# One reduction for the row maxima of both halves, on the ring of bank pairs: a four-layer decoder on one core

## What is computed

```
x = _layernorm(x + stage(x, ctx))
```

```
att = jnp.einsum('bhtd,bhsd->bhts', q, k) / math.sqrt(DH)
w = jax.nn.softmax(att, axis=-1)
```

## Time and profile before

| | |
|---|---|
| median of 3 runs | 1834.8 us (1828.02 to 1838.67) |
| the profiled execution | 1828.59 us, its span 1826.9 us |
| busy PE / DVE / ACT / POOL | 1387.8 / 1102.6 / 704.8 / 365.9 us |
| mean granted TensorE clock | 0.854 |
| DVE reductions of the row maxima (L1355) | 704 instructions, 411.7 us busy |
| exponentials of the pairs (L1766) | 352 instructions, 312.0 us busy |

### The profile page before, as it was taken

One profiled execution on the slowest core, in us unless ns is written; L12 is line 12 of the kernel. 1 busy time (PEld: TensorE's weight loads), 2 busy tenths in 40 slices (PEclk: granted clock), 3 DMA queues, 4 the chain that ended last, 5 costly groups with the idle time before them and its releaser, 6 DMA issues. The chain is left out here.

```text
span 1826.9 us, 25724 instructions
## 1 busy us (share of the span) xinstructions
PE 1387.8 (76%) x9530; PEld 662.0 (36%) x9530; DVE 1102.6 (60%) x2350; ACT 704.8 (39%) x988; POOL 365.9 (20%) x432
## 2 busy tenths in 40 slices
PE   2668888774663676684777998889799899987886
PEld 1333432331330342342233545434344444444443
DVE  3677746778669468667976556664224524256655
ACT  1026654453333213112434452445625435433342
POOL 2415441006105106105531030112301200020000
PEclk6669987886576897696788999999899899988998
DMA  8612113000100210213122142130301401031111
GB/s 186 126 42 54 37 36 70 3 1 1 35 1 1 63 41 24 56 44 63 28 50 50 40 91 58 57 77 2 92 2 35 105 25 59 1 83 41 36 30 45
DMA packets 49784, 86.35 MB, mean 47 GB/s; under 512 B 13686, under 2 KB 42166, under 8 KB 44982
## 3 DMA queue, kind: packets, MB, share of 16 engines
q1 hardware_dynamic: 49662, 84.71, 19.7%
HBM read 66.95 MB, written 15.60 MB: 45 GB/s over the span
## 5 line engine op out<-in xcount | busy, mean ns | idle before, releaser
L1355 DVE TENSOR_REDUCE MX<-ps 128x3 f32<-128x462 f32 (+5 forms) x704 | 411.7, 627 | 215.7 <-PE ps L943 149.0
L1766 ACT ACTIVATE WORK<-ps 128x1024 f32<-128x1024 f32 (+1 forms) x352 | 312.0, 948 | 119.7 <-PE ps L971 82.4
L937 PE MATMUL ps<-KH,QH 48*128 48x154 bf16 (+5 forms) x1536 | 146.6, 279 | 124.6 <-DVE MX L1355 80.3
L1010 PE MATMUL ps<-WORK,VA 128*18 128x512 f32 (+3 forms) x1536 | 167.9, 533 | 4.8 <-ACT WORK L1774 2.0
L937 PEld LDWEIGHTS ps<-KH,QH 48*128 48x128 bf16 (+1 forms) x1536 | 61.3, 99 | 289.4 <-DVE MX L1355 156.7
L971 PE MATMUL ps<-QH,KH 54*128 54x512 bf16 (+3 forms) x768 | 120.6, 368 | 48.0 <-ACT WORK L1766 36.9
L2006 POOL TENSOR_SCALAR_AFFINE_SELECT WORK<-WORK 128x256 f32<-128x256 f32 (+1 forms) x192 | 94.6, 499 | 303.1 <-ACT WORK L1766 302.8
L2016 POOL TENSOR_TENSOR SIDE<-SIDE 128x2048 f32<-128x2048 f32 x16 | 96.5, 6034 | 292.7 <-ACT SIDE L1835 251.4
L1860 ACT ACTIVATE SIDE<-ps 128x512 f32<-128x512 f32 x96 | 57.2, 597 | 248.3 <-PE ps L1131 247.9
L1601 DVE TENSOR_TENSOR SIDE<-SIDE,ps 128x512 f32<-128x512 f32 x96 | 65.8, 687 | 122.4 <-ACT SIDE L1860 122.2
L1137 PE MATMUL ps<-SIDE 128*128 128x128 f32 x768 | 107.7, 285 | 38.8 <-DVE SIDE L1612 19.8
(11 more groups left out here) (270 smaller groups left out, 2180.5 us busy)
## 6 DMA issues: line engine op xcount, KB each, us to landing
SIDE<-in_experts SPq DMA_DIRECT2D x96, 192.0 KB, 2.4
scratch<-HQ SPq DMA_DIRECT2D x48, 192.0 KB, 2.9
QH<-scratch SPq DMA_DIRECT2D x48, 192.0 KB
SIDE<-in_wide SPq DMA_DIRECT2D x8, 1024.0 KB, 6.0
QH<-scratch SPq DMA_DIRECT2D x48, 128.0 KB
scratch<-HK SPq DMA_DIRECT2D x16, 192.0 KB, 2.9
QH<-scratch SPq DMA_DIRECT2D x48, 64.0 KB
KH<-scratch SPq DMA_DIRECT2D x16, 192.0 KB
```

The costliest lines, as they stand in the source:

```text
L937: mms[b] = pe.matmul(banks[b][:, c * pitch:c * pitch + width], qr[b][:, h, t * 128:t * 128 + 128], kr[b][:, h, 0:width], start=(c == 0), s ...
L1010: mm = pe.matmul(ps[32 * j:32 * j + 2 * NV, UB, q0:S], lhsT.rearrange("p a c -> p (a c)"), PB[:, (PAIR_BASE[F] + where[pi]) % NSLOT, b, at ...
L1355: dve.tensor_reduce(MX[:, 32 * b + i0:32 * b + i0 + cnt], src, AX.X, ALU.max, negate=True).then_inc(freed, 1)
L1766: act.activation(PB[:, N % NSLOT, :, lo:hi], wide_banks("pair", F, n)[:, :, lo:hi], ACT.Exp).then_inc(sem("exp_done"), 1)
```

## The change

The two reductions of a fill become one. `max` leaves the narrow ring for the wide one: a fill takes a bank pair, PE signals once, and DVE reduces both banks with one instruction of twice the elements (462 to 924, 512 to 1024, 384 to 768 elements per partition). The narrow ring has 352 x 2 fewer fills, the wide ring 352 more. The planner is told so, and its table of numbers is another.

```diff
-BACKLOG, SWITCH, SOON = 3.90, 0.59, 0.153
+BACKLOG, SWITCH, SOON = 2.22, 0.67, 0.156
...
-          "pair": 2, "wide": -27.3}
+          "pair": 11.8, "wide": -50.4}
...
-            return [("PE", 0.3 + 0.07 * cnt * (3 if L.mask in ("full", "causal") else 1)), ("DVE", 2 * (0.16 + 0.161 * cnt))]
-        return [("PE", 0.45), ("DVE", 2 * (0.16 + 0.134 * cnt * (i0 // HH + 1)))]
+            return [("PE", 0.3 + 0.07 * cnt * (3 if L.mask in ("full", "causal") else 1)), ("DVE", 0.16 + 0.322 * cnt)]
+        return [("PE", 0.45), ("DVE", 0.16 + 0.268 * cnt * (i0 // HH + 1))]
...
-NARROW = ("project", "max", "turn", "out", "mix", "wo", "mean", "q0x", "q0t", "h0t", "h0b", "qkv", "ht", "log", "rank", "w0", "w3",
+NARROW = ("project", "turn", "out", "mix", "wo", "mean", "q0x", "q0t", "h0t", "h0b", "qkv", "ht", "log", "rank", "w0", "w3",
           "dn", "acc", "hid2", "f3", "fk3", "pt3", "fin")
-WIDEK = ("pair", "h0", "gu", "g2", "s3")
+WIDEK = ("max", "pair", "h0", "gu", "g2", "s3")
...
-                banks = [ring("max", F, u), ring("max", F, u + 1)]
+                pairs = wide("max", F, u)
+                banks = [pairs[:, b, :] for b in range(2)]
...
-                for b in range(2):
-                    mms[b].then_inc(ring_filled, 1)
+                mms[1].then_inc(all_wide, 1)
...
-                b, i0, cnt = max_units(L)[u]
-                bank = ring("max", F, u)
-                if L.cross:
-                    src = bank[:, 0:cnt * KP].rearrange("p (c k) -> p c k", k=KP)[:, :, 0:KC]
-                else:
-                    w = 128 * (i0 // HH + 1)
-                    src = bank[:, 0:cnt * w].rearrange("p (c k) -> p c k", k=w)
-                dve.tensor_reduce(MX[:, 32 * b + i0:32 * b + i0 + cnt], src, AX.X, ALU.max, negate=True).then_inc(freed, 1)
+                _, i0, cnt = max_units(L)[u]
+                wide_filled(dve, "max", F, u)
+                pitch, width = (KP, KC) if L.cross else (128 * (i0 // HH + 1),) * 2
+                src = wide_banks("max", F, u)[:, :, 0:cnt * pitch].rearrange("p b (c k) -> p b c k", k=pitch)[:, :, :, 0:width]
+                dst = MX[:].rearrange("p (b i) -> p b i", b=2)[:, :, i0:i0 + cnt]
+                dve.tensor_reduce(dst, src, AX.X, ALU.max, negate=True).then_inc(wide_freed, 1)
```

More of the change, by code:

```diff
@@ L145 @@
 SHAPE, RESHAPE = {"max": 64, "pair": 64, "value": 32}, 0.105
-BACKLOG, SWITCH, SOON = 3.90, 0.59, 0.153
-URGENT = {"x": 38.2, "mean": 35.7, "square": 26.1, "wo": 12.3, "mix": 35.7, "out": -10.5, "copy": 7.6, "turn": 4.3,
-          "split": 47.8, "project": -0.1, "pieces": 9.9, "send": 44.9, "max": 3.5, "hid2": 3.7, "f3": 16, "rank": 25,
[3 rows of a table removed]
-          "pair": 2, "wide": -27.3}
-STAGE_URGENT = {"moe3": -5.8, "L1x": 3.9, "moe1": 13.2, "ffn2": -10.6, "L0a": 3.3, "L2x": -0.9, "L3x": -10.9,
-          "L2a": 0.5, "self3": 47.3, "L0x": -6.8, "ffn0": 7.7, "heads1": 0.1}
-EARLIER = -0.09
+BACKLOG, SWITCH, SOON = 2.22, 0.67, 0.156
+URGENT = {"x": 53, "mean": 26.3, "square": 32.4, "wo": 2.2, "mix": 47.6, "out": -6.5, "copy": 13.1, "turn": 3.2,
+          "split": 67.5, "project": -3.7, "pieces": -13, "send": 33.8, "max": 5.7, "hid2": 1, "f3": 9.2, "rank": 9.6,
[3 rows of a table added]
+          "pair": 11.8, "wide": -50.4}
+STAGE_URGENT = {"moe3": -14.9, "L1x": -0.2, "moe1": 9.3, "ffn2": -22.2, "L0a": 31.5, "L2x": -1.6, "L3x": -8.4,
+          "L2a": -3.7, "self3": 53, "L0x": 5.3, "ffn0": 12, "heads1": -17.4}
+EARLIER = 3.14
 def work(kind, stage, i):
@@ L431, in plan @@
             if kind in NARROW:
-                at = len(narrow) - 3 + (1 if kind in ("max", "w3") else 0)
+                at = len(narrow) - 3 + (1 if kind == "w3" else 0)
                 if at >= 0:
@@ L466, in plan @@
         if kind in NARROW:
-            if kind in ("max", "w3"):
-                narrow.append(freed - (d / 2 if kind == "max" else 0.0))
+            if kind == "w3":
+                narrow.append(freed)
             narrow.append(freed)
@@ L486, in plan @@
         out.append((kind, key, i))
-        if kind == "max":
-            out.append((kind, key, i + 1))
     return fronts, out
@@ L1222, in _ @@
                     project(key, i)
-                elif kind == "max" and i % 2 == 0:
+                elif kind == "max":
                     max_units_of(key, i)
@@ L1347, in max_unit @@
                 L = layer_of(F)
-                b, i0, cnt = max_units(L)[u]
-                bank = ring("max", F, u)
-                if L.cross:
-                    src = bank[:, 0:cnt * KP].rearrange("p (c k) -> p c k", k=KP)[:, :, 0:KC]
-                else:
-                    w = 128 * (i0 // HH + 1)
-                    src = bank[:, 0:cnt * w].rearrange("p (c k) -> p c k", k=w)
-                dve.tensor_reduce(MX[:, 32 * b + i0:32 * b + i0 + cnt], src, AX.X, ALU.max, negate=True).then_inc(freed, 1)
+                _, i0, cnt = max_units(L)[u]
[4 more added lines that the diff above has]
+                dve.tensor_reduce(dst, src, AX.X, ALU.max, negate=True).then_inc(wide_freed, 1)
             def split_maxima(F):
-                consumed(dve, "max", F, len(max_units(layer_of(F))) - 1)
+                wide_consumed(dve, "max", F, len(max_units(layer_of(F))) - 2)
                 def piece(i):
```

## The result

The changed kernel takes **1887.5 us** (median of four, 1881.1 to 1894.5) against 1832.8 for the kernel before beside it on the same chip: a ratio of 1.0298, 95% interval 1.0271 to 1.0324. It is 55 us slower. The forecast was 1848, +13 on the median of 1834.8, with a range from 1808 to 1886: the direction is right, the size is not. The profiled execution took 1887.35 us, at a mean granted clock of 0.849 (0.854 before).

What follows compares the result with a forecast made beforehand. No engine alone was the bound: DVE and dependencies set the pace in slices 8 to 19, PE mostly from 23. Terms -5 - 7 - 19 + 35 + 8 + 5 = +17 on 1828.6 gave 1845.6; with 2 carried, 1848 us, range 1808 to 1886.

Steps and rivals of the forecast that it cites:

- 0.062 us a fill: All 352 fills: one reduction instead of two overlapping halves saves 0.062 us of DVE time each, 22 us in all.
- The -7: The 264 fills outside L0a's three stretches: 16 us less DVE time, of which 7 us is won (bounds 0 and -16).
- The -19: PE's other 76 us of waits for the maxima: a quarter recovered, 19 us (bounds nothing and 60 recovered).
- at half or less: Sign that the forecast is right: PE's waits for the maxima fall to half or less.
- The +8: moe1, batch 0: 11 fills of L1x now come alone behind the experts, costing 8 us (0 to +12).
- The +5: Four L2a fronts: maxima move beside experts and hid2, pairs run alone; nearly even, 5 us lost (0 to +20).
- -5: First front, maxima alone: with two bank pairs the period falls from 1.18 to about 0.96 us, saving 5 us once.
- +35: L0a's three stretches: runs of pairs and maxima lose overlap, 51.2 us each against 39.5, 35 us lost (+19 to +46).
- Its bounds are nothing recovered and 60 recovered: Fills waiting for a pair or gu two back on the wide ring: unseen wait, bounded between 0 and 60 us recovered.
- the way it would most easily fail: The new order beyond three places worked out gains or loses 30 us elsewhere, above all between 300 and 900 us.
- The waits were the cost: Rival, whole kernel: two bank pairs let PE fill while DVE reduces, and the narrow ring is freed; 1795 us, chance 0.22.
- The clock goes too: Rival: clock falls to about 0.75 in L0a's stretches and runs of pairs, +28 us, 1876 us, chance 0.10.

Runs made afterwards that it cites:

- the run with L0a alone: Kernel before, same order, only the 88 units of the first attention layer on the bank pairs with one reduction each: 1855.1 us, ratio 1.0143.
- 1909: The change's bank pairs and single reduction for all 352 fills, with every item in the order of the kernel before: 1909.4 us, ratio 1.0452.
- the late release: Kernel before with its two reductions; in 229 of 352 units the first no longer gives its bank back, the second gives back both: 1890.5 us, ratio 1.0333.
- the 95 fills with two reductions: Kernel before with 95 units, those with maxima as neighbour on each side, on the bank pairs, two reductions each, both banks freed after the second: 1803.7 us.
- 2044: The change's order and table, with the narrow ring and two reductions of the kernel before: 2043.7 us, ratio 1.1162.
- the kernel with 95 fills: Kernel before with 95 of 352 units, those with maxima as neighbour on each side, on the bank pairs with one reduction: 1803.6 us, ratio 0.9866.

## Why the prediction was right and wrong

**Right: the price of the instruction.** The forecast took 0.062 us a fill, 22 us, from the overlap of two halves, and 1224, 1120 and 955 ns. Measured: 0.0625, and 1220, 1113 and 951. DVE's reductions are busy for 373.6 us, not some 390, since part of the fall came with the new order. The Trainium skill's 125 ns for DVE on PSUM (Perfetto Trace Analysis, Optimizing Scalar/DVE Operations) would be, as an estimate, 44 us for 352 instructions; the runs with and without the merge show 22, twice (395.6 to 373.6, and 409.3 to 387.0 at the order of before), so the measurement decides against it.

**Right: three terms behind L0a.** The -7 for DVE's shorter work fits in size the 10 us that the single instruction was worth in the new order. The -19 for PE's waits for the maxima held on its own rows: in the first front they fell from 22.4 to 5.9 us (16 had been set apart for it), everywhere else from 76.3 to 56.2, 20 won back. The sign "at half or less" did not come (62 of 99), but 16 and 19 off the 92 would not have reached it either. The +8 for `moe1`, batch 0, held too: from its first gate matmul to the last reduction of L1x, batch 1, passed 81.3 us before (606.4 to 687.7) and 91.4 in the change (630.6 to 722.0). The +5 for the L2a fronts has no run.

**Mis-sized, and close in sum by luck: L0a.** The third stretch ends 23 us late, where -5 and +35 made 30. The parts were off in opposite ways: the first front ended 21.8 us earlier, not 5 (10.7 of it are the ring's, by the run with L0a alone; the rest is the order's), and the stretches grew by 45, not 35. One part of the 45 was foreseen only as a rival: the clock fell, and PE was busy 22 us longer for eight matmuls more (122 us, 41 a stretch, where the prediction had some 34 as covered). How much of these 22 is on the path no run tells.

**Wrong: what the sum put at nothing.** For all that comes after L0a the sum had -7, -19, +8 and +5, together -13. Measured: +58.7 less 23, that is +35. The step that failed is "Its bounds are nothing recovered and 60 recovered": the fill that waits on the wide ring for a pair or a `gu` two turns back was bounded on the side of gain alone, and the rest of the new order, worked out at three places only, had no term. What the runs showed in its place: at the order of before, that wait and its mirror, a pair that waits for a reduction, come to 88 us in PE's list, and the kernel loses 80 us (1909 against 1829); with every layer but L0a moved it loses 62. The new order avoids most of these waits (15 us are left) and pays with waits of other names. Behind L0a alone, PE waits 28 us more for the keys of a front, 15 more at `mean`, 14 more for the copies of the accumulator and 8 more for exponentials, 20 less for the maxima and 19 less at all other places, and it is busy 9 us longer: +35. At the order of before the shared ring alone raises the first two much less (keys 43 us against 35, `mean` 19 against 15), so they belong to the new order more than to the ring. The prediction had named this as the way it would most easily fail.

**The rivals.** "The waits were the cost" had a true part: with fills moved only where maxima stand in runs, the kernel gets faster, to 1803.6. That this is near its 1795 is a coincidence, since the 1795 counts the new order's loss in L0a, which that kernel doesn't have. For the change it fell: its stretches of L0a are 52 us and more, and 20 of the 76 us came back, not 38. "The clock goes too" (1876) is the nearest in time, and half of its condition came: in the stretches of L0a the clock fell from 0.94 to 0.84, not to 0.75 (PE's share of them was 0.84 before, not the 0.86 that the rival starts from), while behind L0a it is 0.86 in both kernels. The Trainium skill's advice to rotate matmul groups through banks (Perfetto Trace Analysis, Matmuls) agrees with two runs that kept every reduction of before: the late release, for a loss of 60 us, and the 95 fills with two reductions, for a gain of 26.

**The range.** The ends named for the forecast's own range (L0a +25 and +46, the waits -30 and -8, L2a +15) add up to 1827 and 1880 around 1848, not to 1836 and 1878. The result lies above both.

**Open.** Why the change, with few shared turns left, still stands 55 us over the kernel before is told by the list of PE's waits only, not by a run for each. A third bank pair for the wide ring was not tried: with seven banks for both rings it leaves the narrow one a single bank.

## What to carry to other kernels

Before merging two reads of PSUM, count banks, not instructions: how many banks does each producer have before and after, and when does each come free? Here, at a fixed order, the instruction was worth 0 to 10 us of 1830, an early release 60, and moving all maxima to the ring of another user 80. Move a user to a second ring only where it is idle (95 of 352 fills: 27 us faster), and bound an unseen wait on the side of loss as carefully as on that of gain. When a sum covers a new order at three places only, the rest needs a term with bounds of its own. An order tuned for one ring can do badly on another (2044, and 2058 for the old table on the new ring), so compare at a fixed order first.

## What was not expected of the hardware

Merged reductions overlap back to back too. Two groups without a gap, the first from the change, the second from the kernel with 95 fills:

```profile
62.04 9.15 DVE L1351 TENSOR_REDUCE MX<-ps 128x2 f32<-128x1024 f32 x8 [0.59 <-PE ps L942]
```
```profile
92.17 6.14 DVE L1370 TENSOR_REDUCE MX<-ps 128x2 f32<-128x768 f32 x7
```

They take 1.144 and 0.877 us each of the group's time, where one such instruction lasts 1.220 and 0.951 on average (the means of the change): 0.075 us less, more than the 0.0625 that the merge itself saves.
